# Last stage of a post-norm transformer layer: each layer norm's statistics in a group of its own, the inverse root refined on GpSimd

## The reference

```python
def attention(x):                 # x: 4 x 2048 x 256, 16 heads of 16
    q, k, v = split(x @ w_qkv + b_qkv)
    q, k = rope(q), rope(k)       # all but the first tokens
    return softmax(q @ k.T * 0.25) @ v @ w_proj + b_proj

def ffn(x):                       # fp4_linear: x and w quantised in blocks of 16 to E2M1 and back
    gate, y = fp4_linear(x, w_gate), fp4_linear(x, w_up)      # 256 -> 704
    return fp4_linear(silu(gate) * y, w_down)                 # 704 -> 256

def layernorm(x):
    return (x - mean(x)) / sqrt(var(x) + 1e-5)

x = layernorm(x + attention(x))
x = layernorm(x + ffn(x))
```

## Time and profile before

| | us |
|---|---|
| median of 3 runs (lowest, highest) | 3483.42 (3480.58, 3485.93) |
| the profiled execution's own time | 3483.45 |
| its span | 3481.7 |
| PE busy (matmuls) | 3382.2, 97% |
| DVE busy | 3220.4, 92% |
| ACT busy | 2663.9, 77% |
| POOL busy | 761.5, 22% |

### The profile page before, as it was taken

One profiled execution on the slowest core, in us unless ns is written; L12 is line 12 of the kernel. 1 busy time (PEld: TensorE's weight loads), 2 busy tenths in 40 slices (PEclk: granted clock), 3 DMA queues, 4 the chain that ended last, 5 costly groups with the idle time before them and its releaser, 6 DMA issues.

```text
span 3481.7 us, 69112 instructions
## 1 busy us (share of the span) xinstructions
PE 3382.2 (97%) x27752; PEld 1522.8 (44%) x27752; DVE 3220.4 (92%) x3531; ACT 2663.9 (77%) x4946; POOL 761.5 (22%) x871
## 2 busy tenths in 40 slices
PE   8989999999999999999999999999999999999997
PEld 4543333333333333333333333333333347776665
DVE  6778999999999999999999999999999949988887
ACT  5627888888888888888888888888888864444444
POOL 5830110101011001101010110011000026655554
PEclk9968999999999999999999999999999999999999
DMA  4531222222222122111122221122111111211110
GB/s 148 189 109 64 102 93 86 93 93 94 72 89 78 63 82 97 72 61 70 60 89 72 99 82 54 57 79 78 64 69 64 42 55 58 77 48 40 40 34 22
DMA packets 132972, 264.18 MB, mean 76 GB/s; under 512 B 30022, under 2 KB 84518, under 8 KB 114214
## 3 DMA queue, kind: packets, MB, share of 16 engines
q1 hardware_dynamic: 119520, 243.25, 19.9%
q10 hardware_dynamic: 13132, 16.52, 1.4%
HBM read 173.11 MB, written 84.93 MB: 74 GB/s over the span
## 4 chain that ended last, share of the span: by engine, by line
PE 84%; ACT 5%; DVE 3%; DMA 2%; issue 2%; POOL 2%; SPq 0%; ACTq 0%; POOLq 0%; DVEq 0%
PE ps L681 36%; PE ps L734 32%; PE ps L817 8%; PE ps L829 4%; ACT arena L942 2%; DMA qst<-qk_parts 1%; PE ps L744 1%; PE ps L721 1%; PE ps L652 1%; ACT arena L917 1%; POOL arena L1296 1%; DVE arena L1083 1%; ACT v_all L990 1%; POOL arena L1305 0%; ACT arena L980 0%
## 5 line engine op out<-in xcount | busy, mean ns | idle before, releaser
L1083 DVE TENSOR_REDUCE arena<-ps 128x1 f32<-128x1024 f32 x2048 | 2495.8, 1222 | 59.9 <-PE ps L681 43.2
L942 ACT ACTIVATE arena<-ps 128x512 f32<-128x512 f32 x4096 | 2222.1, 596 | 321.2 <-PE ps L721 235.8
L681 PE MATMUL ps<-kst,qst 48*128 48x512 f32 x4096 | 1520.3, 452 | 13.9 <-DVE arena L1083 10.8
L721 PE MATMUL ps<-qst,kst 51*128 51x512 f32 x4096 | 1498.2, 448 | 0.2
L734 PE MATMUL ps<-arena 128*32 128x256 f32 x16384 | 1309.3, 392 | 16.8 <-ACT arena L917 15.9
L681 PEld LDWEIGHTS ps<-kst,qst 48*128 48x128 f32 x4096 | 614.6, 188 | 870.3 <-DVE arena L1083 698.9
L734 PEld LDWEIGHTS ps<-arena 128*32 128x32 f32 x16384 | 327.3, 108 | 739.5 <-issue 409.0
L721 PEld LDWEIGHTS ps<-qst,kst 51*128 51x128 f32 x4096 | 608.8, 185 | 15.5 <-ACT arena L942 12.2
L1360 POOL TENSOR_TENSOR arena<-arena,ones 128x16 bf16<-128x16 f32 x64 | 14.2, 222 | 2305.0 <-DVE arena L1088 2305.0
L817 PE MATMUL ps<-wgT,arena 128*128 128x352 f32 x512 | 195.5, 464 | 15.5 <-ACT arena L932 15.5
L829 PE MATMUL ps<-wdT,arena 128*128 128x256 f32 (+1 forms) x768 | 181.1, 385 | 17.5 <-ACT arena L980 16.3
(11 more groups left out here) (104 smaller groups left out, 2073.8 us busy)
## 6 DMA issues: line engine op xcount, KB each, us to landing
qk_parts<-arena SPq DMA_DIRECT2D x32, 1024.0 KB, 5.9
kst<-qk_parts SPq DMA_DIRECT2D x127, 256.0 KB
qst<-qk_parts SPq DMA_DIRECT2D x127, 256.0 KB
qk_whole<-arena SPq DMA_DIRECT2D x16, 1024.0 KB, 4.6
arena<-qk_whole SPq DMA_DIRECT2D x16, 1024.0 KB, 5.1
kst<-qk_parts SPq DMA_DIRECT2D x127, 128.0 KB
qst<-qk_parts SPq DMA_DIRECT2D x127, 128.0 KB
att<-arena SPq DMA_DIRECT2D x256, 34.0 KB
```

The costliest lines, as they stand in the source:

```text
L681: mm = nc.tensor.matmul(ps[:, i % S_BANKS, :], q[SROW:SROW + STACK, qt * P:(qt + 1) * P], k[SROW:SROW + STACK, kc * CHUNK:(kc + 1) * CHUNK ...
L721: nc.tensor.matmul(ps[:, bank_of_t(g.c, i), :], kst[g.u % 2][first:first + ROWS, kb * P:(kb + 1) * P], qst[g.u % 2][first:first + ROWS, qb ...
L942: nc.scalar.activation(pt[kb % 2][:, qb * CHUNK:(qb + 1) * CHUNK], ps[:, bank_of_t(g.c, i), :], ACT.Exp).then_inc(p_ready, 1)
L1083: nc.vector.tensor_reduce(mx[g.u % 2][:, i // 2, i % 2:i % 2 + 1], ps[:, bank:bank + 2, :].rearrange("p b t -> p (b t)"), AX.X, ALU.max).t ...
```

## The change

The two residuals' groups are no longer merged. `variance` takes its columns and semaphores as arguments and is called as `variance1` right behind `residual1` (lag 2) and as `variance2` behind `residual2` (lag 10); each is six small instructions on four columns. `inverse_std` is gone from DVE: `inverse_root` on POOL takes the power and then does the Newton step itself, six instructions in all, each waiting for the one before it. It is called as `inverse_root1` at the beginning of POOL's step and as `inverse_root2` behind `round_h`. `norm1` waits for `ln1_step`, `norm2` for `ln2_step`. The factor -0.5 of the shift moves from the last instruction into `sums`, on DVE. In the first call, inside the last head, `variance1` is followed by `residual1` of tile 4 with no `inverse_std` between them.

```diff
--- before.py
+++ after.py
@@ -183,14 +183,9 @@
     return g * TILES_S + i + AHEAD >= (G - 1) * TILES_S
 
 
-def norm_group(n, alone):
...
+def group_of(n):
+
+    return n if n.u == 3 else None
 
 
 def each_head(fn):
@@ -355,7 +350,8 @@
         pv_step, v_staged, o_out, inverted = (sem(n) for n in ("pv_step", "v_staged", "o_out", "inverted"))
 
         proj_psum, y_done, y_step = (sem(n) for n in ("proj_psum", "y_done", "y_step"))
-        var_step, root_done, ln_step, x1_done = (sem(n) for n in ("var_step", "root_done", "ln_step", "x1_done"))
+        var1_step, root1_done, ln1_step, x1_done = (sem(n) for n in ("var1_step", "root1_done", "ln1_step", "x1_done"))
+        var2_step, root2_done, ln2_step = (sem(n) for n in ("var2_step", "root2_done", "ln2_step"))
         q_max, q_small, x_scaled, h_scaled, x_power, h_power, xq_step = (sem(n) for n in (
             "q_max", "q_small", "x_scaled", "h_scaled", "x_power", "h_power", "xq_step"))
         x_steady, h_steady = (sem(n) for n in ("x_steady", "h_steady"))
@@ -917,7 +913,7 @@
                 nc.scalar.activation(ost[g.u % 2], ps[:, O_BANK, :], ACT.Copy).then_inc(o_out, 1)
 
             def norm1(n):
-                act.wait_ge(ln_step, n.quad(LN_STEPS, LN_STEPS))
+                act.wait_ge(ln1_step, n.quad(LN_STEPS, LN_STEPS))
                 wait_after(act, y2_done, n.times(1, 1 - LONG))
                 nc.scalar.activation(x1_r[n.c % LONG], y_r[n.c % LONG], ACT.Identity, bias=shift[:, n.u:n.u + 1],
                                      scale=rstd[:, n.u:n.u + 1]).then_inc(x1_done, 1)
@@ -960,7 +956,7 @@
 
 
             def norm2(n):
-                act.wait_ge(ln_step, n.quad(LN_STEPS, 3 * LN_STEPS))
+                act.wait_ge(ln2_step, n.quad(LN_STEPS, LN_STEPS))
                 wait_after(act, out_st[n.u], n.quad(16))
                 nc.scalar.activation(o_r[n.u], y2_r[n.c % LONG], ACT.Identity, bias=shift[:, 4 + n.u:5 + n.u],
                                      scale=rstd[:, 4 + n.u:5 + n.u]).then_inc(o_done, 1)
@@ -1097,52 +1093,32 @@
             invert_sums(At(0, G - 4))
 
 
-            def variance(n, alone):
...
+            def variance(n, cols, stats, stepped, refined):
+
+                e = group_of(n)
+                if not e:
                     return
                 at = lambda k: e.quad(VAR_STEPS, k)
                 g_bn, g_var, g_sums, g_d = bn[:, cols], var[:, cols], sums[:, cols], ln_d[:, cols]
+                dve.wait_ge(stats, e.times(1, 1))
+                wait_after(dve, refined, e.quad(LN_STEPS))
+                nc.vector.tensor_tensor(g_d, g_bn[:, :, 1], g_bn[:, :, 4], ALU.subtract).then_inc(stepped, 1)
+                nc.vector.tensor_tensor(g_var, g_bn[:, :, 2], g_bn[:, :, 5], ALU.add).then_inc(stepped, 1)
+                dve.wait_ge(stepped, at(1))
+                nc.vector.scalar_tensor_tensor(out=g_sums, in0=g_d, scalar=-0.5, in1=g_bn[:, :, 4],
+                                               op0=ALU.mult, op1=ALU.subtract).then_inc(stepped, 1)
+                dve.wait_ge(stepped, at(3))
+                nc.vector.tensor_tensor(g_d, g_d, g_d, ALU.mult).then_inc(stepped, 1)
+                nc.vector.tensor_scalar(g_var, g_var, 1.0 / C, EPS, ALU.mult, ALU.add).then_inc(stepped, 1)
+                dve.wait_ge(stepped, at(5))
                 nc.vector.scalar_tensor_tensor(out=g_var, in0=g_d, scalar=0.25, in1=g_var,
-                                               op0=ALU.mult, op1=ALU.add).then_inc(var_step, 1)
-
-            def inverse_std(n, alone):
...
+                                               op0=ALU.mult, op1=ALU.add).then_inc(stepped, 1)
+
+            def variance1(n):
+                variance(n, slice(0, 4), y_step, var1_step, ln1_step)
+
+            def variance2(n):
+                variance(n, slice(4, 8), y2_step, var2_step, ln2_step)
 
             def residual1(n):
                 dve.wait_ge(proj_psum, n.times(1, 1))
@@ -1261,17 +1237,15 @@
 
             for n in range(4):
                 residual1(At(0, n))
-            variance(At(0, 3), False)
-            inverse_std(At(0, 3), False)
+            variance1(At(0, 3))
             residual1(At(0, 4))
             invert_sums(At(0, G - 3))
             quantise_xh(At(0, 0))
             residual1(At(0, 5))
             quantise_xh(At(0, 1))
             run_straight(TILES, [
-                (2, residual1, 6), (3, lambda n: inverse_std(n, False), 4), (11, lambda n: inverse_std(n, True)),
-                (6, quantise_xh, 2), (8, quantise_last_h), (10, residual2),
-                (2, lambda n: variance(n, False), 4), (10, lambda n: variance(n, True)), (7, silu_up), (8, late_sums)])
+                (2, residual1, 6), (2, variance1, 4), (6, quantise_xh, 2), (8, quantise_last_h), (10, residual2),
+                (10, variance2), (7, silu_up), (8, late_sums)])
 
 
         @block.gpsimd
@@ -1401,15 +1375,37 @@
                     rounded(hh_r[n.u][:, cols], hs_r[p][:, cols], q_sc[p][:, HB.start + hf * nb:HB.start + (hf + 1) * nb], hr_step,
                             n.times(2, hf + 1), hq_done, nb)
 
-            def inverse_root(n, alone):
-                if group := norm_group(n, alone):
-                    e, cols = group
-                    pool.wait_ge(var_step, e.quad(VAR_STEPS, VAR_STEPS))
-                    wait_after(pool, ln_step, e.quad(LN_STEPS))
-                    nc.gpsimd.tensor_tensor(std[:, cols], var[:, cols], power[:, cols], ALU.pow).then_inc(root_done, 1)
-
-            run_straight(TILES, [(6, round_x), (2, lambda n: inverse_root(n, False)), (10, lambda n: inverse_root(n, True)),
-                                 (8, round_h), (8, late_job)])
+            def inverse_root(n, cols, rooted, stepped, refined):
+
+                e = group_of(n)
+                if not e:
+                    return
+                sd, r, s = std[:, cols], rstd[:, cols], shift[:, cols]
+                u = ln_t[:, cols]
+                def link(k, ins):
+                    ins.then_inc(refined, 1)
+                    pool.wait_ge(refined, e.quad(LN_STEPS, k))
+                pool.wait_ge(stepped, e.quad(VAR_STEPS, VAR_STEPS))
+                nc.gpsimd.tensor_tensor(sd, var[:, cols], power[:, cols], ALU.pow).then_inc(rooted, 1)
+                pool.wait_ge(rooted, e.quad(1, 1))
+                link(1, nc.gpsimd.tensor_tensor(u, sd, sd, ALU.mult))
+                link(2, nc.gpsimd.tensor_tensor(u, u, var[:, cols], ALU.mult))
+                link(3, nc.gpsimd.tensor_scalar(u, u, -0.5, 1.5, ALU.mult, ALU.add))
+                if cols.start == 0:
+                    wait_after(pool, x1_done, e.times(1, -3))
+                else:
+                    wait_after(pool, o_done, e.times(1, -3))
+                link(4, nc.gpsimd.tensor_tensor(r, sd, u, ALU.mult))
+                nc.gpsimd.tensor_tensor(s, sums[:, cols], r, ALU.mult).then_inc(refined, 1)
+
+            def inverse_root1(n):
+                inverse_root(n, slice(0, 4), root1_done, var1_step, ln1_step)
+
+            def inverse_root2(n):
+                inverse_root(n, slice(4, 8), root2_done, var2_step, ln2_step)
+
+            run_straight(TILES, [(2, inverse_root1), (6, round_x), (8, round_h), (10, inverse_root2), (8, late_job)])
```

More of the change, by code:

```diff
@@ L1124, in inverse_std @@
-            def inverse_std(n, alone):
-                group = norm_group(n, alone)
-                if not group:
-                    return
-                e, cols = group
-                sd, t, r = std[:, cols], ln_t[:, cols], rstd[:, cols]
-                def link(k, ins):
-                    ins.then_inc(ln_step, 1)
-                    dve.wait_ge(ln_step, e.quad(LN_STEPS, k))
-                dve.wait_ge(root_done, e.quad(1, 1))
-                if cols.start == 0:
-                    wait_after(dve, x1_done, e.times(1, -3))
-                if cols.stop == 8:
-                    wait_after(dve, o_done, e.back(8).times(1, -3))
-                link(1, nc.vector.tensor_tensor(t, sd, sd, ALU.mult))
-                link(2, nc.vector.tensor_tensor(t, t, var[:, cols], ALU.mult))
-                link(3, nc.vector.tensor_scalar(t, t, -0.5, 1.5, ALU.mult, ALU.add))
-                link(4, nc.vector.tensor_tensor(r, sd, t, ALU.mult))
-                nc.vector.scalar_tensor_tensor(out=shift[:, cols], in0=sums[:, cols], scalar=-0.5, in1=r,
-                                               op0=ALU.mult, op1=ALU.mult).then_inc(ln_step, 1)
+                dve.wait_ge(stats, e.times(1, 1))
```

20 lines of the change are left out of this document (removed).

## The result

The changed kernel takes **3499.13 us** (median of 6 runs, 3493.75 to 3506.12), the kernel before 3480.56 us beside it (6 runs, 3478.64 to 3485.93): ratio 1.0051, 95% interval 1.0036 to 1.0066. It is slower by 18.6 us of medians, 16.9 us of spans (3498.6 against 3481.7), where +19.7 was forecast. The forecast of the total is met, its terms less well: each group cost less than predicted, the start and the end more.

The account below looks back on a forecast made before the run. The prediction took PE to be the bound, with norm2's scale coming later from POOL. Eleven groups 10.8, four with a late job 8.2, start 0 and end 0.7 gave +19.7 us: 3503 us, range 3490 to 3516.

Parts of the forecast that it names:

- What bounds the kernel: Last stage: PE is the bound; every fourth step costs 1.03 us extra, waiting for norm1's scale, norm2, then L932.
- step 2: Second step of a group of four tiles, by PE's transposes: 10.59 us before, forecast 11.5, about 12.6 in four groups.
- Root 1: First residual's power and refinement, a step earlier: norm1 stops waiting, DVE's work behind variance 1 comes 0.9 us later.
- Root 2: Second residual's power and refinement on POOL behind round_h: norm2 comes 0.98 us later, in 11 groups 10.8 us.
- Steps with a late job: Four groups where POOL's L1353 holds variance 1's small DVE instructions: 1.06 us more each, with the 0.98 8.2 us.
- Start: First group, only the first residual's root: wait goes, variance 1 meets round_h; taken as 0, bounds -1.6 and +2.5.
- End: Last norm2 chain, where nothing hides the second residual's root on POOL: +0.7 us.
- What was to be seen: Profile signs: step lengths, norm2 waiting for L1399, power directly behind round_h, variance 2 over 2 to 3 us, links 0.30.
- The sum: Whole kernel: 10.8, 8.2, start 0 and end 0.7 make +19.7 us, 3503 us; bounds +3, +34 and +46.
- Rival A: Faster: norm2's root ready in time if round_h ends by 3136.4, no step waits; -15 us, 3468 us; chance 0.10.
- B: No change: links at 0.20 us, variance 2 not held, norm2 0.3 us or less later; +5 us, 3488 us; chance 0.10.
- C: DVE becomes the bound through held small instructions of 3 us and more; some 23 us on top, 3526 us; chance 0.04.

Follow-up runs that it names:

- e6: Changed kernel with variance 1 and inverse_root1 left out from the second group on, so not the whole layer: 3479.80 us, ratio 0.9989 to the kernel before.
- e8: Changed kernel with inverse_root2 ahead of round_h, late jobs at lag 9, second group's variance1 and inverse_root1 moved later: 3482.53 us, ratio 0.9998 to the kernel before.
- e9: Changed kernel with inverse_root2 ahead of round_h, second group's variance1 and inverse_root1 moved later, late jobs at lag 8: 3465.70 us, ratio 0.9950 to the kernel before.
- e2: Changed kernel with POOL's eight late jobs one step later (lag 9 for 8): 3498.64 us, ratio 1.0047 to the kernel before.
- e1: Changed kernel with inverse_root2 ahead of round_h on POOL, all else alike: 3471.88 us, ratio 0.9973 to the kernel before.
- e7: Changed kernel with five more dependent small POOL instructions in inverse_root2, values unchanged: 3552.09 us, ratio 1.0203 to the kernel before.
- e4: Changed kernel with inverse_root2's Newton step on DVE at the next step's head, power still behind round_h on POOL: 3496.05 us, ratio 1.0036 to the kernel before.
- e3: Kernel before, groups still merged, with its Newton step on POOL directly behind the power: 3471.92 us, ratio 0.9965 to the kernel before.

## Why the prediction was right, point by point

**What bounds the kernel: right.** PE, and in step 2 norm2, L928, gate products, in that order.

**Root 1: right.** Variance 1 ran from 3136.39 to 3137.17, where L1157 follows: 0.78 us, and round_x came 0.88 us late (forecast 0.9). e6 gives the same 0.89. Root 1 itself costs nothing, though its last two links are held by DVE (0.48 and 0.73 us): POOL still waits 0.83 us for ACT before round_x (row at 3141.35).

**Root 2: right in mechanism, each group's size too large.** "Norm2 comes 0.98 us later than before": it came 0.56 later (1.66 after the transposes against 1.10). POOL's round_x and round_h took 5.55 us (3141.35 to 3146.90), forecast 5.54, and the power 1.01. Three terms were too long: "the last one at 3138.4 + 0.17", since variance 2 was through at 3146.06, before POOL's last instruction began (one or two of its six ran at each end of POOL's, not one), 0.17; the hand-over to the power, 0.07, was nothing; and five links took 1.32 us instead of 1.50, as they stand 0.28 apart and the last needs only its own 0.20. Together 0.42, to within the 0.05 us of the rows. The wait of 0.7 us for PE's projection did not come: its L740 starts at 3147.86, right behind the transposes. "I take 0.30, since 16 elements are nearly the same as 4" was right to 0.02.

**Steps with a late job: right**, 1.03 us each instead of 1.06, by the mechanism given (one small instruction of 1.24 us), and e6 shows that nothing else is in it. There the Trainium skill, "SBUF — State Buffer", section "Who interferes with whom", agrees with the rows: a DVE instruction with two inputs in SBUF is held until POOL's ends (L1106, 1.24 us beside L1327's 1.29), and a reduction is not (L1157 takes 0.42 us beside POOL's power at 3137.31).

**Start: mis-sized**, +0.58 and not 0. The named meeting of variance 1 with round_h happened (L1108 0.86 and L1112 0.76 us). It was worth 0.6 us net in the changed kernel, but it hid a possible gain: with that group's variance 1 out of the way (e8, e9) the pair of steps is 0.6 us under that of the kernel before (21.01 against 21.65) and 1.2 us under the changed kernel's 22.22.

**End: mis-sized.** For the last group in the end and the last root the prediction had 0.98 + 0.7 = 1.7 us; it was 4.0. A stall of PE was priced at its own length: the lower clock behind 2.30 us of idle time cost 1.70 us more, and DVE held the links, so that the stall itself was 1.77 us longer than before and not 0.98. The 1.70 us might as well have stayed away, as they did in e2.

**What was to be seen.** Of the signs named, norm2 waiting for L1399, root 2 directly behind round_h, variance 2 spread over 2.3 us on DVE (3143.73 to 3146.06) and variance 1 under 1 us all showed; the step of 11.5 us was 11.16, that of 12.6 with a late job 12.19, and the links' 0.30 was 0.28.

**The sum.** Forecast 10.8 + 8.2 + 0 + 0.7 for the 15 groups and the end. Measured, in the same cut: ten ordinary steps 5.5, four with a late job 6.4, start 0.6, end with its group 4.0, and 0.4 ahead of the stage. So 16.9 met 19.7 because 6.1 us too much in fourteen groups stood against 3.3 too little around them. That part is luck: the direction and the path were right for the reason given, the closeness was not earned. The upper bound of +34 was also added up short: it has the late jobs' 4.3 us but neither the start's own +2.5 nor the end's 1.5, which make it +38 or so.

**Rival A** named the right condition, round_h out of the way, and e1 made it true: its last stage is 8.3 us shorter than that of the kernel before, where A gave 15. The difference is the four late jobs, 3.8 us, which A left out, and the start, where A counted a gain of 1.2 and e1 lost 2.2, 1.6 of them by the clock. B, no change, failed although links did cost less, C by the 9.56 us of all other steps.

## What to carry to other kernels

A short dependent chain that another engine waits for belongs directly behind its input on a free engine, and ahead of every long instruction whose own deadline is later; which engine runs it matters less (here 0.4 us a group against 1.6 for the place). When an instruction is moved by one step, look at all that waits in order behind its semaphore, the DMA queue included, and at what it will now run beside, as DVE and POOL held each other here. And compare the stage that was edited by itself: of 7.8 us between two medians here, 7.1 were not in it.

## What the hardware showed that was not expected

- **A stall of PE can cost more than its length, or not.** Behind an idle time of 2.30 us (changed kernel, tile 63), 2.40 (e2, tile 59) or 3.67 (e7, 2947.52) PE ran about 3 us at the lower level, a granted clock of 0.50 or 0.51, and pairs of products took up to 1.54 us instead of 0.76. Behind 2.30 us in e2, 2.40 in the changed kernel and 3.26 in e7 (2904.72) they did not. The 2.47 us or so at the start, the same in six profiles, were followed by it in e1 and e4 alone. What decides was not found; length alone does not.
- **The holding goes both ways.** POOL's instructions on four columns, 0.20 us alone, take 0.48 to 0.74 us beside DVE's L1167 and L1171, as DVE's small ones do beside POOL's.
- **A power on four columns is 1.01 us, on eight 1.64** (e3), but a product is 0.20 us on either: splitting the group cost 0.38 us in powers, nothing in width for the rest.
